# Encoder feed-forward of two units gathered at one place of a two-slot schedule

## The reference

```python
for i in range(4):                                   # encoder, 16 heads of 8
    xn = layer_norm(x, ln1_w[i], ln1_b[i])
    x = x + mha(xn, mask, ...)                       # causal + ALiBi, softmax over 256 keys
    xn = layer_norm(x, ln2_w[i], ln2_b[i])
    h = gelu(xn @ ffn1_w[i].T + ffn1_b[i], approximate=False)   # 128 -> 512
    x = x + (h @ ffn2_w[i].T + ffn2_b[i])                       # 512 -> 128
return layer_norm(x, final_w, final_b)
```

## Time and profile before

| | us |
|---|---|
| three timed runs | 1691.81, 1693.17, 1693.47 |
| median | 1693.17 |
| the profiled execution, its own time | 1682.76 |
| its span, first to last instruction | 1680.9 |

### The profile page before, as it was taken

One profiled execution on the slowest core, in us unless ns is written; L12 is line 12 of the kernel. 1 busy time (PEld: TensorE's weight loads), 2 busy tenths in 40 slices (PEclk: granted clock), 3 DMA queues, 4 the chain that ended last, 5 costly groups with the idle time before them and its releaser, 6 DMA issues.

```text
span 1680.9 us, 38344 instructions
## 1 busy us (share of the span) xinstructions
PE 1426.3 (85%) x10656; PEld 943.5 (56%) x10720; DVE 1130.3 (67%) x2851; ACT 1224.1 (73%) x2165; POOL 622.8 (37%) x1052
## 2 busy tenths in 40 slices
PE   0677777479999999999999999999999989899995
PEld 0445544246666666666666665666666655566663
DVE  6577766257766676666776666777666667777762
ACT  3233333158888888888888888888888888888884
POOL 5233332224333333333333333333333335455543
PEclk9699999689999999999999999999999999999997
DMA  3333332254554444555544454444454444444430
GB/s 106 95 114 95 99 108 82 58 131 115 124 122 113 116 123 127 133 119 118 117 113 113 113 120 130 113 116 119 117 119 119 113 130 120 119 119 122 129 94 10
DMA packets 134765, 187.61 MB, mean 112 GB/s; under 512 B 19912, under 2 KB 110696, under 8 KB 134696
## 3 DMA queue, kind: packets, MB, share of 16 engines
q1 hardware_dynamic: 119880, 150.45, 35.7%
q0 software_dynamic: 14848, 36.74, 8.0%
HBM read 120.87 MB, written 65.01 MB: 111 GB/s over the span
## 4 chain that ended last, share of the span: by engine, by line
PE 36%; DMA 19%; DVE 17%; issue 15%; SPq 6%; POOL 2%; DVEq 1%; ACT 1%; POOLq 0%; ACTq 0%
DMA blocks<-split_L 16%; PE pvp L973 8%; PE mxp L917 7%; DVE negm L692 7%; PE exp_ps L950 5%; PE dense L862 4%; PE mxp L921 3%; DVE xn L660 3%; SPq L361 3%; PE dense L991 2%; SPq L385 2%; PE dense L890 2%; PE dense L1003 2%; DVE stats L646 1%; DVE negt L732 1%
## 5 line engine op out<-in xcount | busy, mean ns | idle before, releaser
L825 ACT ACTIVATE probs<-exp_ps 128x512 f32<-128x512 f32 x896 | 525.8, 593 | 322.6 <-PE exp_ps L950 321.1
L692 DVE TENSOR_REDUCE negm<-mxp 128x2 f32<-128x512 f32 x896 | 568.9, 681 | 136.2 <-remote 87.1
L917 PE MATMUL mxp<-blocks,qst 104*128 104x512 f32 x768 | 328.3, 457 | 70.3 <-DMA blocks<-split_L 55.0
L950 PE MATMUL exp_ps<-qbd_l,kst_l 128*128 128x512 f32 x768 | 368.9, 496 | 8.6 <-issue 4.7
L849 ACT ACTIVATE exp_ps<-masktf 128x512 f32<-128x512 f32 x513 | 308.8, 602 | 23.1 <-DVE rest L760 7.0
L492 POOL TENSOR_SCALAR veps<-mv 128x2 f32<-128x2 f32 x144 | 31.7, 220 | 591.9 <-DVE mv L651 588.2
L921 PE MATMUL mxp<-maskb,identb 128*128 128x256 bf16 (+1 forms) x704 | 223.0, 317 | 0.0
L917 PEld LDWEIGHTS mxp<-blocks,qst 104*128 104x128 f32 x768 | 149.5, 195 | 127.5 <-issue 47.8
L973 PE MATMUL pvp<-probs,vst_l 128*32 128x256 f32 (+1 forms) x4096 | 194.4, 330 | 0.6 <-ACT probs L825 0.6
L738 DVE COPY ost<-pvp 128x512 f32<-128x512 f32 x80 | 55.3, 692 | 201.6 <-PE pvp L973 201.6
L950 PEld LDWEIGHTS exp_ps<-qbd_l,kst_l 128*128 128x128 f32 x768 | 144.5, 195 | 41.2 <-issue 31.6
(11 more groups left out here) (95 smaller groups left out, 1995.1 us busy)
## 6 DMA issues: line engine op xcount, KB each, us to landing
split_L<-hi SPq DMA_DIRECT2D x256, 128.0 KB, 2.1
qst<-split_L SPq DMA_DIRECT2D x64, 384.0 KB
kst_l<-split_L SPq DMA_DIRECT2D x64, 384.0 KB
qbd_l<-split_L SPq DMA_DIRECT2D x256, 96.0 KB
split_L<-lo POOLq DMA_DIRECT2D x128, 128.0 KB, 2.1
blocks<-split_L SPq DMA_DIRECT2D x128, 96.0 KB
blocks<-split_L POOLq DMA_DIRECT2D x128, 96.0 KB, 4.1
split_F<-hi SPq DMA_DIRECT2D x64, 128.0 KB, 2.1
```

The costliest lines, as they stand in the source:

```text
L692: dve.tensor_reduce(negm[:, s, qt, h0:h0 + count], mxp[:, (plan.max_chunks * g + ch) % 3, :].rearrange("p (h t) -> p h t", h=count), AX.X, ...
L825: act.activation(probs[:, g[0], ch, :], exp_ps[:, (plan.exp_chunks * g[0] + ch) % 2, :], ACT.Exp, scale=plan.scale).then_inc(q.b_exp, 1)
L917: pe.matmul(mxp[:, bank, :], qst[0:BIAS_END, g[0], qt * P:(qt + 1) * P], kbd[0:BIAS_END, g[0], first:first + count, 0:keys], start=True, s ...
L950: pe.matmul(exp_ps[:, bank, :], kst[plan.name][:, s, g[0], kt * P:(kt + 1) * P], rhs, start=not on_diagonal, stop=True, skip_group_check=T ...
```

## The change

The order of the encoder's steps now differs between even and odd slots. At the end of an even slot s stand `f1` and the gelus of unit s-2 and of unit s-1, with `pv` 2 between them. At the head of the odd slot s after it stand `f2` of unit s-3 and of unit s-2, behind `max` 0 and `max` 1. The odd slot has no `f1`, the even slot no `f2`. The maxima stand behind `exp` 3 to 9 in the even slot and in the head and behind `exp` 2 to 7 in the odd one; `negt` and the restack for the maxima come after `exp` 11 in the even slot and after `exp` 9 in the odd one. `xt` comes ahead of the maxima in the even slot. In the last layer `end`, `end+` and `store` of both units stand in the odd slot. `f2` of an even unit uses bank `dense[1]`, of an odd one `dense[0]`, and `at` moves from `dense[0]` to `dense[1]`.

```diff
--- before.py
+++ after.py
@@ -63,7 +63,7 @@
         self.stack_dmas = self.hg + 1 if causal else self.hg // 2 + 1
         self.max_dmas, self.pool_dmas = self.hg // 2 + 1, self.hg // 2
         self.units = 2 * rounds
-        self.at_bank = 0 if causal else 1
+        self.at_bank = 1
 
     def max_bank(self, ch):
 
@@ -82,21 +82,36 @@
         maxes = [("max", s + 1, *divmod(k, self.max_chunks)) for k in range(self.max_chunks * GROUPS)]
         values = [("pv", s, g) for g in range(GROUPS)]
 
-        if self.causal:
-            end, end2, store = (at(k, s - 2) if last_layer else [] for k in ("end", "end+", "store"))
+        if self.causal and s % 2 == 0:
             return (
                 exps[0:2] + at("ot", s - 1) + at("ln", s + 2) + at("ot+", s - 1) + at("v v+", s + 1) + at("xn", s + 2)
-                + at("f2 f2+", s - 2) + at("at at+", s - 1)
-                + exps[2:3] + maxes[0:2] + at("xt", s + 2)
-                + exps[3:4] + maxes[2:4] + at("xt+", s + 2) + at("op", s - 1) + at("stack+", s + 1)
-                + exps[4:5] + maxes[4:5] + at("op+", s - 1) + at("qk", s + 2)
-                + exps[5:6] + maxes[5:7] + at("qk+", s + 2)
-                + exps[6:7] + maxes[7:9] + at("xn2", s - 1) + end
-                + exps[7:8] + maxes[9:11]
-                + exps[8:9] + maxes[11:12]
-                + exps[9:10] + at("xt2 xt2+", s - 1) + values[0:2] + end2
-                + exps[10:11] + at("negt negt+", s + 1) + at("stack_max+", s + 2)
-                + exps[11:12] + at("f1 f1+", s - 1) + values[2:4] + at("pv+", s) + store)
+                + at("at at+", s - 1)
+                + exps[2:3] + at("xt", s + 2)
+                + exps[3:4] + maxes[0:2] + at("xt+", s + 2) + at("op", s - 1) + at("stack+", s + 1)
+                + exps[4:5] + maxes[2:4] + at("op+", s - 1) + at("qk", s + 2)
+                + exps[5:6] + maxes[4:6] + at("qk+", s + 2)
+                + exps[6:7] + maxes[6:8]
+                + exps[7:8] + maxes[8:9] + at("xn2", s - 1)
+                + exps[8:9] + maxes[9:10]
+                + exps[9:10] + maxes[10:12] + at("xt2 xt2+", s - 1)
+                + exps[10:11] + values[0:2]
+                + exps[11:12] + at("negt negt+", s + 1) + at("stack_max+", s + 2) + at("f1 f1+", s - 2)
+                + values[2:3] + at("f1 f1+", s - 1) + values[3:4] + at("pv+", s))
+        if self.causal:
+            end, end2, store = (at(k, s - 3) + at(k, s - 2) if last_layer else [] for k in ("end", "end+", "store"))
+            return (
+                exps[0:2] + at("ot", s - 1) + at("ln", s + 2) + at("ot+", s - 1) + at("v v+", s + 1) + maxes[0:1]
+                + at("xn", s + 2) + at("f2 f2+", s - 3) + maxes[1:2] + at("f2 f2+", s - 2) + at("at at+", s - 1)
+                + exps[2:3] + maxes[2:4] + at("xt", s + 2)
+                + exps[3:4] + maxes[4:6] + at("xt+", s + 2) + at("op", s - 1) + at("stack+", s + 1)
+                + exps[4:5] + maxes[6:7] + at("op+", s - 1) + at("qk", s + 2)
+                + exps[5:6] + maxes[7:9] + at("qk+", s + 2) + end
+                + exps[6:7] + maxes[9:11] + at("xn2", s - 1)
+                + exps[7:8] + maxes[11:12]
+                + exps[8:9] + end2
+                + exps[9:10] + at("negt negt+", s + 1) + at("stack_max+", s + 2) + values[0:2]
+                + exps[10:11] + at("xt2 xt2+", s - 1)
+                + exps[11:12] + values[2:4] + at("pv+", s) + store)
         return (
             at("ot", s - 1) + at("ln", s + 2) + at("ot+", s - 1) + at("xn", s + 2) + exps[0:2] + at("at at+", s - 1)
             + at("v v+", s + 1) + at("xt", s + 2)
@@ -783,7 +798,7 @@
                     elif step == "f2+":
                         dve.wait_ge(q.c_f2, u + 1)
                         dve.wait_ge(q.c_xb2, u + 1)
-                        dve.tensor_tensor(state[:, bt, :, :], dense[1][:, 0:T].rearrange("p (t d) -> p t d", t=NT),
+                        dve.tensor_tensor(state[:, bt, :, :], dense[1 - s][:, 0:T].rearrange("p (t d) -> p t d", t=NT),
                                           xb2[:, s, :, :], ALU.add).then_inc(q.c_done, 1)
 
             rounds_of(dve, EXPERT, lambda n: steps(EXPERT, n))
@@ -1006,10 +1021,10 @@
                             last.then_inc(q.c_f1, 1)
                     elif step == "f2":
                         pe.wait_ge(q.c_gelu, NF * (u + 1))
-                        dense_job(1, q.c_done, 1, off + BATCH)
+                        dense_job(1 - s, q.c_done, 1, off + BATCH)
                         for t in range(NT):
                             for f in range(NF):
-                                last = pe.matmul(dense[1][:, t * D:(t + 1) * D], hid[:, s, f, t * P:(t + 1) * P],
+                                last = pe.matmul(dense[1 - s][:, t * D:(t + 1) * D], hid[:, s, f, t * P:(t + 1) * P],
                                                  wc["L"][:, C_W2 + f * D:C_W2 + (f + 1) * D], start=(f == 0),
                                                  stop=(f == NF - 1))
                         last.then_inc(q.c_f2, 1)
```

## The result

| | before | after |
|---|---|---|
| median of 4 timed runs | 1692.49 | 1841.31 |
| lowest, highest | 1687.52, 1693.47 | 1838.33, 1847.34 |
| span of the profiled execution | 1680.9 | 1836.6 |

The ratio is 1.089, with a 95% interval of 1.0851 to 1.0929: 149 us slower. The prediction was 1857 with a range of 1755 to 1915.

The account below looks back on a forecast made before the run. A ring of waits, once per slot, was taken to set the period, PE fitting in. 31 pairs by (4.7 - 0.1), plus 18 and 3, gave +164 us: profiled 1682.76 to 1847, plus 10.4 for the median, 1857; range 1755 to 1915.

Parts of the forecast that it names:

- the ring: Once per slot: first maximum to `hi`, `hi` to restack, restack to next first maximum; mean 20.3 us, setting the period.
- Table loads at nothing: On ACT, four loads fewer before and two after per pair: 2.57 us less ACT work, taken to gain nothing.
- Odd slot, first link: From first maximum to `hi` in odd slots: both `f2` now inside, so `hi` at 11.3 us in place of 6.6.
- Odd slot, its end: Next first maximum after an odd slot's: 24.6 to 25.4 us by the restack, about 24.4 by PE alone.
- the 6.9 from `hi` to the restack: In the odd slot, DMA issues of `hi` and `lo` and their DRAM writes before the restack: 6.9 us, as before.
- 13.46 and 13.46: In the kernel before, first maximum to restack: 13.46 us through `negt`, the same as through `hi`.
- Even slot: From its first maximum to the next: 19.9 to 20.6 us, mean 20.2, 0.1 less than before; `negt` decides.
- the last link: From the restack to the next first maximum, in the even slot: 6.43 to 7.15 us.
- The rival: Granted clock falls at every odd slot's end, 31 pairs by 1.6 us more, +49: 1906 us; chance 15%.
- a granted clock clearly below 1.00: Sign of being wrong: the granted clock in the encoder clearly below 1.00 in the profile after.
- Last layer: Doubled `end` and `end+` in odd slots delay the restack 2.9 us, eight times: +18 us net, between 0 and 35.
- Sum: Over the whole run: 31 pairs give 143 us, with 18 for the last layer and 3 for the tail, +164.

Follow-up runs that it names:

- Even order: The kernel before, nothing gathered, with the changed kernel's even-slot order in every slot: 1662.84 us, ratio 0.9851; once more 1665.71 us, ratio 0.9854.
- The kernel with the filler: The changed kernel with six idle bf16 products added on PE in each odd slot, where PE waits anyway: 1837.01 us, ratio 1.0864 to the kernel before.
- The first experiment: The changed kernel with both second products of the odd slot moved ahead of the first maximum: 1827.89 us, ratio 1.0818 to the kernel before.
- the kernel gathered on the order of before: The kernel before's order in both slots, with first products of two units in even slots and second products in odd ones: 1871.56 us, ratio 1.1083.

## Why the prediction was right, step by step

- **Bound.** Right: the ring sets the period, and neither PE's busy share nor ACT's. In the odd slots it closes over PE's own steps and their short waits, no longer over the restack. Even order against before and the kernels without gelu show both halves of it.
- **Table loads at nothing.** Right, by experiment: 3 us for all of them in the kernel before, and nothing in the one after. The Trainium skill's advice to do all of one table set before switching (ScalarE: Activation LUTs, Rules for kernel authors) saves ACT's time, and ACT's time did fall here, by 75 us; it just wasn't what the slot waited for.
- **Odd slot, first link.** Predicted `hi` at 11.3, measured 11.46; `negt` 14.7 and 14.91. The seven reductions and the statistics behind the two second products make it up as worked out.
- **Odd slot, its end.** Predicted 24.6 to 25.4 by the restack and 24.4 by PE alone. Plain slots at the full clock are 24.8, and it is PE alone that ends them. One step failed without harm, the 6.9 from `hi` to the restack: it is 5.93 here (561.63 to 567.57 on SP). I had read the 6.85 of before as the time that the `lo` parts need. It was the time until SP got past `negt+`, which came just behind it. Where two ways round give the same number, as 13.46 and 13.46 did, the trace can't tell which one it is a property of.
- **Even slot.** Predicted 20.2, measured 19.25 on average. Two terms were mis-sized. `negt` comes at 10.99, not 11.7, for the second normalisation takes 0.60 and not 1.12 (below). And the last link takes 6.0 on average from the restack, not 6.8.
- **Clock.** The rival had 15% and its event in every pair at +1.6. It came in part: in 8 of the 18 odd slots without weight loads ahead of the last layer, at 1.4 each, with waits half as long as the only example I had; also in three of the five with weight loads and in every odd slot of the last layer. The forecast had nothing for it. The mean odd slot (25.96 in 23) is 1.2 above the plain one at the full clock, of which the eight slots make 0.5 and the slots with weight loads the rest. I had named a granted clock clearly below 1.00 as a sign of being wrong: over the full slots it is 0.97, for 1.00 before.
- **Last layer.** Predicted near 28, measured 27.96 on average, by another way than I had. I had the restack end these slots, 2.9 later for the `end` operations. On SP it does leave late, 9.9 after `hi` in place of 5.9, and POOL's share (L570) in the longest of these slots leaves at 1578.15, 13.9 after `hi` at 1564.29, behind two `end` and `end+` chains. But in this profile PE waits for the restack at the end of only one of the seven. It waits 2.27 for the last reduction, which stands behind the `end` statistics on DVE, so that `negt` comes at 16.08 and not 14.92. In the longest slot it also waits for the transfer of `negt`, whose copy on DVE stands behind `end+`. PE, then POOL, in that slot:

```profile
1568.90 0.59 PE L877 MATMUL dense<-ident,negm 128*16 128x128 f32 x2 [2.27 <-DVE negm L707]
...
1578.11 1.22 PE L965 MATMUL exp_ps<-qbd_l,kst_l 128*128 128x512 f32 x2 [2.02 <-DMA qbd_l<-negt]
```

```profile
1577.28 0.72 POOL L537 TENSOR_TENSOR fo<-tmp,rest 128x256 f32<-128x256 f32 x1 [0.31 <-POOL tmp L532]
1578.15 1.29 POOL L570 DMA_DIRECT2D blocks<-split_L  x2
```

  Behind the 2.27 the clock falls too. The kernel with the filler tells what that is worth: four of its last six odd slots keep the full clock and take 27.1 to 27.4 all the same, and now the chain of waits ends in the restack:

```profile
1612.55 0.49 POOL blocks L570
...
1613.24 3.73 DMA blocks<-split_L
...
1617.01 0.50 PE mxp L932
```

  So PE at the lower clock and the restack are equally long here, and I had worked out only one of the two.
- **Sum.** +164 predicted; +149 by the medians, +156 by the profiled spans (pairs 142, the rest 14 ahead of the first and behind the last full slot, where I had 3). The median lies 2.9 above the profiled execution in the kernel after, where I had added 10.4, which makes the difference between the two. With the last layer in it I had the odd slot at 25.6 on average and it is 26.43; I had the even one at 20.2 and it is 19.25. So the pair came out right (5.2 more predicted with the last layer, 4.7 measured) partly by two errors that cancel. Ahead of the last layer a pair takes 4.5 more, for 4.6 predicted, but of that plain slots at the full clock make only 3.4; the lower clock makes 0.5 and the slots with weight loads and their neighbours 0.6, and I had neither. The mechanism was right; that the size fits so closely is luck in part.

**Why gathering costs what it does** is only half in the prediction, which saw the cost in the place behind the first maximum. The first experiment corrects that: with both second products ahead of it a pair of plain slots still takes 43.2 us at the full clock, for 43.9 in the change. Each slot has some 8 us under its restack where PE can do work that nobody waits for. Before, each held one first and one second product, 3.6 us. Gathering puts two first products under the even slot's restack, and then both second products have to be done either there too, where they no longer fit (even slot 22.0 to 24.3 at the full clock), or behind the first maximum, where they push `hi` (odd slot 24.8). Under the odd slot's restack nothing is left to do, and PE waits (2.36 us in the kernel gathered on the order of before, 4.15 in pieces in the change); behind such waits the clock fell in all the gathered kernels, in some slots or in most. Spreading the second products over both slots wasn't tried: `f2` of unit 15 of a layer has to be ahead of `op` in the odd slot after it, since the weights of the next layer go into the same buffer.

## What to carry to other kernels

Find the ring first: the events that repeat in the chain of waits, and how long each link is. An edit is worth what it does to a link, whichever engine is busiest; and the cover under a transfer is a resource of each turn, so work gathered into one turn overflows there and leaves the next one idle. Before saving an overhead, replace it by nothing in a throw-away kernel: here the one with the identity for gelu prices all the loads at 3 us. Sort the slots by the granted clock before averaging them: a slot that is 1.4 or 1.6 us longer may be the same slot at the lower clock. Where two paths in the trace have the same length, take neither for the bound until an experiment has lengthened one.

## What the hardware showed beyond that

- **A normalisation on DVE is held until POOL's `lo` is done.** The second normalisation, two instructions on DVE, takes 1.20 us in the kernel before and 0.60 in the even slots of the one after. The instructions are the same. In the odd slot they take 1.19 again. What differs is when POOL forms `lo`: in the slow ones it still has some 0.9 us to go when the first of the two starts, in the fast one 0.3 us. In all 60 slots of the kernel before in which the first one starts beside `lo` (0.94 us long, for 0.34 alone), and in all 54 of the one after, it ends 0.08 to 0.10 us after `lo` does. So it isn't slowed in proportion; it ends when POOL has. The reductions that run wholly beside `lo` take their usual 0.68. The timelines of DVE and POOL, the even slot and then the odd one:

```profile
539.12 0.60 DVE L675 TENSOR_SCALAR xn<-state,mv,rstd 128x128 f32 x2
...
563.16 1.19 DVE L675 TENSOR_SCALAR xn<-state,mv,rstd 128x128 f32 x2
```

```profile
538.11 1.28 POOL L541 TENSOR_TENSOR lo<-y,hi 128x512 fp32r<-128x512 f32 x1
...
562.75 1.27 POOL L541 TENSOR_TENSOR lo<-y,hi 128x512 fp32r<-128x512 f32 x1
```

  The even order profits from it: it moves the normalisation behind `exp` 7, past `lo`. The Trainium skill (GPSIMD Engine Reference, Specifications) says that the two engines share SBUF interfaces and contend there when DVE runs in a two-port mode or reads two tensors from SBUF; a normalisation that ends only after `lo` agrees with it. That this sharing is the cause was not tested by itself: no run moved `lo` alone.
- **The clock falls after waits shorter than I thought.** One wait of 2.2 us did it before; in the change two waits of 0.65 and 1.1 us with work between them do, in some slots and not in others of the same shape. Longer waits don't always do it either: in the kernel gathered on the order of before, five even slots that follow waits of 0.65 to 2.6 us kept the full clock.
